# Attention with one filler per head pair on TensorE instead of one per half pair, and score maxima ten pairs ahead

## The chip, the core and the metric

The kernel runs on one core of one Trainium2 chip. The time is the device time of one execution in microseconds (us). The engines of the core run side by side, each through its own list of instructions in order, and wait for one another on semaphores: TensorE (PE; its weight loads are listed as PEld), VectorE (DVE), ScalarE (ACT), GpSimd (POOL) and SyncE (SP), which here only issues DMAs.

## The reference, cut to what matters

The input is x, 32 batches of 256 tokens of width 128. One layer of attention plus a mixture of experts:

```python
xl = _layer_norm(x, ln_l_g, ln_l_b)
xg = _layer_norm(x, ln_g_g, ln_g_b)
# local: attention among the first 32 tokens of each batch (zero for the others)
# glb:   attention among all 256 tokens of each batch
# both: 16 heads of width 8, softmax(q k^T), then times v, then w_out
x = _layernorm(x + (local + glb))
x = _layernorm(x + moe(x))    # top-1 of 8 experts, hidden 512, capacity 1024
```

So the local part is a block of 32 rows for each batch (LW = 32).

## The kernel before

**Units and steps.** The attention is cut into 36 units of 256 query rows: units 0 to 3 are the local part (the 32-row blocks of eight batches each, kept apart by a mask), units 4 to 35 are one batch each. Two units share their input projections; such a pair (18 of them) is projected two pairs ahead. A step u works on unit u, and the program runs steps 0 to 39; the last four only empty the pipeline, and then the experts run (`experts`).

**Head pairs.** The 16 heads of a unit are eight head pairs, hp = 0 to 7, and each pair has two halves e = 0, 1: two heads whose q and k lie in partitions 0 to 63 and 64 to 127. Scores are computed twice. `max_pass` (L513) makes q k^T into `ps_a` (one bank for each e), whose row maxima VectorE takes (`take_max`, L942). `exp_pass` (L536) makes k q^T into `ps_b` with the maximum already subtracted (as extra rows of the operands), ScalarE takes the exponential (`exponential`, L760), and `p_v` (L562) multiplies by v into `ps_o`. q and k are held as sums of bf16 parts stacked to 48 rows, written to memory (`store_stacks`, L329) and read back per unit into `qs` and `ks` (`load_stack`, L358), which have two buffers of 8 pairs each, loaded in halves of four pairs.

**The way of the maxima.** In step u TensorE makes the exponential scores of unit u and the maximum scores of unit u + 1. After four pairs VectorE's maxima are split by GpSimd (`split_max`), turned by TensorE (`turn_max`, L572), copied by ScalarE (`copy_max`, L767, semaphore `mT_ready`) and placed into `qs` by SyncE's DMAs (`place_max`, L384, semaphore `max_rows`); `exp_pass` of pairs 0 and 4 waits for `max_rows`.

**The order on TensorE is written by hand.** Each step is 16 half slots: `score_half(u, hp, e)`, that is two `exp_pass` and two `max_pass` matmuls (which run two at a time, on rows 0 to 63 and 64 to 127 of the array), and then `fill(u, hp, e)`, one piece of other work. The fillers are: `p_v` (a piece of 4 matmuls) after both halves of hp 0, 2, 4 and 6; `turn_x` or `project_in` (inputs of a coming pair) at hp 1 and 5 with `turn_max`; `count_tokens`, `turn_o` at hp 3; `turn_oN`, `turn_x1`, `logits`, `project` at hp 5 and 7. Even steps carry `turn_x` and q, odd steps k and v of the same pair. `max_pass` of a half waits for `take_max` of the pair before in the same half, `exp_pass` for exponentials one or two pairs back.

**The other engines** follow hand-written lists per step too: `fill` on VectorE before each `take_max`, `step` on ScalarE, GpSimd and SyncE. SyncE's list per step before the change is: second half of unit u + 1's stack (4 DMAs), on even steps `store_stacks` (6 DMAs, after waiting for `part2_ready`), `place_max(u, 1)`, `load_xr`, `store_o1` or `store_y`, on even steps `load_x`, first half of unit u + 2's stack (4 DMAs), `place_max(u + 1, 0)`.

## Time and profile before

| | us |
|---|---|
| median of 3 runs (800.12 to 804.97) | 800.67 |
| the profiled execution | 797.34 |
| its span, first to last instruction | 795.4 |
| start of step 0's first exponential | 47.17 |
| steps 0 to 3 (local units) | 47.17 to 109.41 |
| steps 4 to 31 | 109.41 to 570.80 |
| steps 32 to 35 | 570.80 to about 626 |
| emptying and experts | about 626 to 795.4 |
| step 10, step 11 | 15.63, 15.81 |
| step 4, step 8 | 20.53, 22.41 |

A step is counted here from the start of ScalarE's exponential of its pair 0 to that of the next step. Busy shares of the span: PE 87%, PEld 44%, DVE 72%, ACT 62%, POOL 62%. A row of the timeline is: start, duration, engine, line, operation, output<-inputs, shapes, count of merged instructions, and in brackets idle time before it and who ended it. Durations include the instruction's own latency, so the distance between two starts is often shorter than a duration.

### The profile page before, as it was taken

The page shows a single profiled execution, that of the slowest core. Times are in us where ns is not written, and L with a number is a line of the kernel's source. Part 1 is how long each engine was busy: PE and PEld are TensorE (multiplying, and loading weights), DVE is VectorE, ACT ScalarE, POOL GpSimd, SP SyncE. Part 2 cuts the span into 40 slices and gives each one's busy share as a digit, 9 for nine tenths or more (in the row PEclk, how much of TensorE's full clock was granted, in tenths as well). Part 3 has the DMA queues.
Part 4 walks back from the last instruction along what each step waited for, and adds up shares of the span by engine and source line. Part 5 has one row for each costly group of instructions (what it writes and reads, how often), then busy time and mean ns, then how long its engine had stood idle before and what let it go on. Part 6 is the DMA issues. An engine that isn't in the chain of part 4 may idle for free.

```text
span 795.4 us, 19345 instructions
## 1 busy us (share of the span) xinstructions
PE 695.3 (87%) x6502; PEld 351.7 (44%) x6502; DVE 572.3 (72%) x1714; ACT 489.4 (62%) x883; POOL 490.7 (62%) x1004
## 2 busy tenths in 40 slices
PE   1579779898999999899999999999999729999991
PEld 1334333343444444344444444444433415777771
DVE  5555577685888989789888888888887311666664
ACT  1335456585777878678787778787877505344340
POOL 3232324556687877777777768775756650666666
PEclk9755898997999999999999999999999858999996
DMA  4632576756254353352543434525431110343321
GB/s 114 173 107 61 160 193 149 200 137 188 77 166 156 97 174 108 120 176 73 178 145 105 160 104 145 163 70 161 147 95 45 36 57 23 101 132 96 97 73 36
DMA packets 145778, 95.36 MB, mean 120 GB/s; under 512 B 14404, under 2 KB 137885, under 8 KB 145680
## 3 DMA queue, kind: packets, MB, share of 16 engines
q1 hardware_dynamic: 139824, 85.35, 37.0%
q0 software_dynamic: 4096, 7.81, 2.9%
q10 hardware_dynamic: 1760, 0.96, 0.6%
q8 instruction: 53, 0.87, 0.5%
q14 instruction: 45, 0.37, 0.2%
HBM read 47.70 MB, written 45.74 MB: 117 GB/s over the span
## 4 chain that ended last, share of the span: by engine, by line
PE 65%; SPq 13%; DMA 6%; issue 5%; POOL 4%; DVE 4%; ACT 3%; POOLq 0%; ACTq 0%; DVEq 0%
PE ps_b L536 16%; PE ps_o L562 15%; SPq L329 6%; PE ps_a L1382 6%; PE ps_b L1376 5%; SPq L358 4%; DMA qs<-mT 4%; PE ps_f L477 3%; PE ps_f L482 3%; PE ps_f L472 2%; SPq L384 2%; DVE mx L942 2%; POOL out L1496 2%; PE ps_m L572 2%; PE ps_m L606 2%
## 5 line engine op out<-in xcount | busy, mean ns | idle before, releaser
L942 DVE TENSOR_REDUCE mx<-ps_a 128x2 f32<-128x512 f32 (+1 forms) x576 | 374.7, 657 | 109.6 <-PE ps_a L513 102.5
L760 ACT ACTIVATE prob<-ps_b 128x1024 f32<-128x1024 f32 (+1 forms) x288 | 280.7, 975 | 102.5 <-PE ps_b L536 95.0
L536 PE MATMUL ps_b<-qs,ks 59*128 59x256 bf16 (+1 forms) x1152 | 223.3, 276 | 25.7 <-DMA qs<-mT 22.9
L513 PE MATMUL ps_a<-ks,qs 56*128 56x256 bf16 (+1 forms) x1152 | 223.3, 278 | 7.9 <-DVE mx L942 5.0
L562 PE MATMUL ps_o<-prob,vp 128*32 128x256 f32 (+1 forms) x2304 | 183.7, 393 | 0.0
L536 PEld LDWEIGHTS ps_b<-qs,ks 59*128 59x128 bf16 x1152 | 67.0, 95 | 186.2 <-issue 112.2
L1236 POOL DMA_INDIRECT routed<-row,slot x64 | 67.2, 1051 | 31.9 <-issue 26.6
L1496 POOL DMA_INDIRECT out<-res,dest x64 | 64.6, 1010 | 34.2 <-DVE res L1471 19.1
L1172 POOL CAST mpart<-mx 128x16 bf16<-128x16 f32 x72 | 14.0, 194 | 115.2 <-DVE mx L942 114.7
L562 PEld LDWEIGHTS ps_o<-prob,vp 128*32 128x32 f32 x2304 | 46.8, 111 | 61.1 <-issue 54.1
L513 PEld LDWEIGHTS ps_a<-ks,qs 56*128 56x128 bf16 x1152 | 65.2, 96 | 13.4 <-DVE mx L942 8.9
L1421 ACT ACTIVATE prob<-ps_b,b_sb 128x512 f32<-128x512 f32 x48 | 33.0, 687 | 60.2 <-PE ps_b L1376 58.6
L767 ACT COPY mT<-ps_m 24x256 bf16<-24x256 bf16 x72 | 26.0, 361 | 59.2 <-PE ps_m L572 58.8
L1382 PE MATMUL ps_a<-w_sb,prob 128*128 128x128 f32 x512 | 59.6, 276 | 0.0
L1382 PEld LDWEIGHTS ps_a<-w_sb,prob 128*128 128x128 f32 x512 | 58.4, 192 | 0.5 <-issue 0.5
L1154 POOL TENSOR_SCALAR xh<-xt,fmv,frstd 128x128 f32<-128x128 f32 x64 | 50.1, 793 | 1.7 <-issue 0.2
L1209 POOL TENSOR_SCALAR row<-y,mv,rstd 128x128 f32<-128x128 f32 x64 | 50.8, 794 | 0.1
L1376 PE MATMUL ps_b<-xT,w_sb 128*128 128x512 f32 x96 | 46.3, 621 | 0.0
L1452 DVE SCALAR_TENSOR_TENSOR z<-ps_a,rows_sb,xb 128x128 f32<-128x128 f32 x64 | 18.1, 345 | 33.4 <-PE ps_a L1382 33.4
L1186 POOL TENSOR_TENSOR xr<-xr,bo_sb 128x256 f32<-128x256 f32 x36 | 26.1, 724 | 21.7 <-DMA xr<-x 21.6
L1161 POOL TENSOR_TENSOR part<-rest,part 128x512 bf16<-128x512 f32 x32 | 36.4, 1159 | 0.0
L1198 POOL TENSOR_TENSOR rstd<-veps,powm 128x4 f32<-128x4 f32 x32 | 33.3, 1041 | 2.7
(125 smaller groups left out, 1047.8 us busy)
## 6 DMA issues: line engine op xcount, KB each, us to landing
qs<-q_stack SPq DMA_DIRECT2D x144, 96.0 KB
ks<-k_stack SPq DMA_DIRECT2D x144, 96.0 KB
q_stack<-part SPq DMA_DIRECT2D x18, 384.0 KB, 3.0
k_stack<-part SPq DMA_DIRECT2D x18, 384.0 KB, 3.5
q_stack<-part SPq DMA_DIRECT2D x18, 256.0 KB, 3.1
k_stack<-part SPq DMA_DIRECT2D x18, 256.0 KB, 3.6
routed<-empty SPq DMA_DIRECT2D x8, 520.0 KB, 5.7
rows_sb<-routed SPq DMA_DIRECT2D x16, 260.0 KB, 3.8
```

Of the source, the lines that this page charges most:

```text
L329: sp.dma_start(stack[p, :, t0:t0 + n, :], src).then_inc(stack_stored[p % 2], 16)
L513: ins = nc.tensor.matmul(ps_a[:, e, qt * S:qt * S + keys.stop - keys.start], qs[half, h, hp, qt * P:(qt + 1) * P], ks[half, h, hp, keys], ...
L536: ins = nc.tensor.matmul(ps_b[:, exp_bank(hp, e), kt * n:(kt + 1) * n], ks[half, u % 2, hp, kt * P:(kt + 1) * P], qs[half, u % 2, hp, quer ...
L562: last = nc.tensor.matmul(ps_o[32 * j:32 * j + 32, col:col + n], vp[:, u % 6, kt, 4 * q + j, :], prob[:, hp, at:at + n], start=(q % 2 == 0 ...
L760: nc.scalar.activation(prob[:, hp, 0:2 * n].rearrange("p (a n) -> p a n", a=2), src, ACT.Exp).then_inc(exp_done, 1)
L942: nc.vector.reduce_max(mx[:, u % 2, :, col], ps_a[:, e].rearrange("p (t k) -> p t k", t=2)[:, :, 0:k], axis=AX).then_inc(max_done, 1)
L1154: last = nc.gpsimd.tensor_scalar(xh[:, p % 2, t], xt[:, p % 3, t], fmv[:, p % 2, t, 0:1], frstd[:, t:t + 1], ALU.subtract, ALU.mult)
L1209: last = nc.gpsimd.tensor_scalar(row[:, g % 3, t, 0:D], y[:, u % 2, t], mv[:, t, 0:1], rstd[:, 0, t:t + 1], ALU.subtract, ALU.mult)
L1236: pool.indirect_dma_start(out=routed, out_offset=bass.IndirectOffsetOnAxis(ap=slot[:, g % 3, t:t + 1], axis=0), in_=row[:, g % 3, t, :], i ...
L1376: nc.tensor.matmul(ps_h[f], w1_sb[:, he, f * P:(f + 1) * P], xT[:, hk], start=True, stop=True).then_inc(hidden, 1)
L1382: last = nc.tensor.matmul(ps_y[:, bank, t * D:(t + 1) * D], hT[:, hk, f, t * P:(t + 1) * P], w2_sb[:, he, f], start=(f == 0), stop=(f == F ...
L1496: pool.indirect_dma_start(out=out_rows, out_offset=bass.IndirectOffsetOnAxis(ap=dest[:, h, t:t + 1], axis=0), in_=res[:, h, t], in_offset= ...
```

## The change

What it does:

- TensorE: a slot is a whole pair, two `score_half` (8 matmuls) and then one `fill(u, hp)`, which holds the work of two or three of the old fillers. `p_v` pieces are spread over slots 0, 1, 3, 4, 5, 6.
- The maxima run `LEAD = 10` pairs ahead instead of 8, so `max_pass` and `take_max` of unit u + 2's pairs 0 and 1 lie in step u's slots 6 and 7. `qs` and `ks` have three buffers; `load_stack(u + 2)` brings a whole unit in one piece (four DMAs of 192 KB instead of twice four of 96 KB).
- SyncE: `place_max(u, 1)` comes first in a step, then the stack of unit u + 2; `store_stacks` goes to the end of the odd step, behind `place_max(u + 1, 0)`.
- The first half of k is projected in the even step's slot 7, the second half in the odd step's slot 0. `turn_max(u, 1)` is in slot 1, `turn_o` in slot 2, `turn_max(u + 1, 0)` in slot 3, `count_tokens` in slot 5, `turn_oN` and `turn_x1` in slot 6.
- `copy_oNT` and `copy_x1T` are one copy of 512 columns, `copy_turned`. `count_tokens` uses bf16 operands (four matmuls), `queue_places` on GpSimd has two links in place of four, row numbers are set once and moved on by one small instruction.
- VectorE: `norm_o` follows `invert_denominators` in hp 3; the input statistics of a pair are split over an odd and the next even step; other small pieces move by a half slot. ScalarE and GpSimd lists are reordered to match.

```diff
+LEAD = 10
-    qs = sb("qs", [P, 2, NH // 2, S], BF16)
-    ks = sb("ks", [P, 2, NH // 2, S], BF16)
+    qs = sb("qs", [P, 3, NH // 2, S], BF16)
+    ks = sb("ks", [P, 3, NH // 2, S], BF16)
...
+        def load_stack(u):
+
+            b, h, p = u % 3, u % 2, u // 2
+            wait(sp, scores, 8 * (u - 2))
             sp.wait_ge(stack_stored[p % 2], 96 * (p // 2 + 1))
...
         def step(u):
             p = first_pair(u)
-            if there(u + 1):
-                load_stack(u + 1, 1)
-            if u % 2 == 0 and u >= 2 and u // 2 + 1 < NPAIR:
-                store_stacks(u // 2 + 1)
             if there(u):
                 place_max(u, 1)
+            if there(u + 2):
+                load_stack(u + 2)
...
+            if there(u + 1):
+                place_max(u + 1, 0)
+            if u % 2 == 1 and (u + 1) // 2 + 1 < NPAIR:
+                store_stacks((u + 1) // 2 + 1)
...
         def score_half(u, hp, e):
 
+            n = 8 * u + hp + LEAD
             for t in range(2):
                 if there(u):
                     exp_pass(u, hp, 1 - e, t)
-                if there(u + 1):
-                    max_pass(u + 1, hp, e, t)
+                if there(n // 8):
+                    max_pass(n // 8, n % 8, e, t)
...
+        def fill(u, hp):
+
+            first, second = first_pair(u), second_pair(u)
+            if hp == 0:
+                if there(u - 1):
+                    p_v(u - 1, 2, 1)
+                    p_v(u - 1, 3, 0)
+                if second is not None:
+                    project_in(second, "k", 1)
+            if hp == 1:
+                if there(u - 1):
+                    p_v(u - 1, 3, 1)
+                if first is not None:
+                    turn_x(first, 0)
+                    turn_x(first, 1)
...
         for u in range(U + 4):
             for hp in range(8):
-                for e in range(2):
-                    score_half(u, hp, e)
-                    fill(u, hp, e)
+                score_half(u, hp, 0)
+                score_half(u, hp, 1)
+                fill(u, hp)
...
+        def copy_turned(u):
+
+            first, end = (0 if there(u - 1) else S), (2 * S if routes(u - 2) else S)
+            if there(u - 1):
+                act.wait_ge(oN_turned, u)
+                wait(act, projected, u - 1)
+            if routes(u - 2):
+                act.wait_ge(x1_turned, batch(u - 2) + 1)
+                wait(act, logits_ready, batch(u - 2))
+            nc.scalar.copy(turned_T[:, first:end], ps_m[:, first:end]).then_inc(turned_copied, 1)
```

How it moves instructions at three places. First TensorE in an even step of the global units, before: two half slots of one pair and the score matmuls ahead of the second.

```order
L536 MATMUL ps_b<-qs,ks 128x256 [waits exp_done]
L513 MATMUL ps_a<-ks,qs 128x256 [waits max_done]
L536 MATMUL ps_b<-qs,ks 128x256
L513 MATMUL ps_a<-ks,qs 128x256
L562 MATMUL ps_o<-prob,vp 32x256 [waits exp_done]
L562 MATMUL ps_o<-prob,vp 32x256 x3
L536 MATMUL ps_b<-qs,ks 128x256 [waits exp_done]
L513 MATMUL ps_a<-ks,qs 128x256 [waits max_done]
L536 MATMUL ps_b<-qs,ks 128x256
L513 MATMUL ps_a<-ks,qs 128x256
L562 MATMUL ps_o<-prob,vp 32x256 x4
```

And after the change, slot 0 of an even step (L530 is `exp_pass`, L507 `max_pass`, L557 `p_v`).

```order
L530 MATMUL ps_b<-qs,ks 128x256 [waits exp_done,max_rows0]
L507 MATMUL ps_a<-ks,qs 128x256 [waits max_done]
L530 MATMUL ps_b<-qs,ks 128x256
L507 MATMUL ps_a<-ks,qs 128x256
L530 MATMUL ps_b<-qs,ks 128x256 [waits exp_done]
L507 MATMUL ps_a<-ks,qs 128x256 [waits max_done]
L530 MATMUL ps_b<-qs,ks 128x256
L507 MATMUL ps_a<-ks,qs 128x256
L557 MATMUL ps_o<-prob,vp 32x256 x4
L557 MATMUL ps_o<-prob,vp 32x256 [waits exp_done]
L557 MATMUL ps_o<-prob,vp 32x256 x3
```

The two score groups now stand together and the two `p_v` pieces too.

Second SyncE, before, from the middle of an odd step to the middle of an even one (L358 stack loads, L384 the maxima's rows, L329 stack stores).

```order
L358 DMA qs<-q_stack 48x4x256 x2
L358 DMA ks<-k_stack 48x4x256 x2
L384 DMA qs<-mT 3x4x256 x2
L358 DMA qs<-q_stack 48x4x256 x2
L358 DMA ks<-k_stack 48x4x256 x2
L329 DMA q_stack<-part 128x3x512
L329 DMA q_stack<-part 128x2x512
L329 DMA q_stack<-part 128x512
L329 DMA k_stack<-part 128x1536
L329 DMA k_stack<-part 128x1024
L329 DMA k_stack<-part 128x512
L384 DMA qs<-mT 3x4x256 x2
```

After, from the head of an odd step (L380 the maxima's rows, L355 stack loads, L328 stack stores).

```order
L380 DMA qs<-mT 3x4x256 x2
L355 DMA qs<-q_stack 48x8x256 x2
L355 DMA ks<-k_stack 48x8x256 x2
L372 DMA xr<-x_local 32x128
L373 DMA xr<-x 96x128
L374 DMA xr<-x 128x128
L400 DMA out<-o 128x2x128
L380 DMA qs<-mT 3x4x256 x2
L328 DMA q_stack<-part 128x3x512
L328 DMA q_stack<-part 128x2x512
L328 DMA q_stack<-part 128x512
L328 DMA k_stack<-part 128x1536
```

The rows of the maxima no longer stand behind loads and stores; the loads stand behind them.

Third ScalarE in an odd step, before, between the exponentials of pairs 2 and 4 (L735 is `second_part`).

```order
L772 COPY oT<-ps_o 128x512 [waits o_turned,pv_done]
L816 COPY count<-ps_m 128x32 [waits places_ready,counted]
L760 ACTIVATE prob<-ps_b 128x1024 [waits pv_done,scores]
L735 CAST part<-rest 128x2x512 [waits rest_k,rest_q]
L802 COPY row<-tokid 128x2 [waits tok_moved,scattered2]
L804 ACTIVATE tokid<-tokid 128x2 [waits row_numbered]
L760 ACTIVATE prob<-ps_b 128x1024 [waits pv_done,scores]
```

After (L772 is the exponential, L779 `copy_max`, L746 `second_part`).

```order
L784 COPY oT<-ps_o 128x512 [waits o_turned,pv_done]
L779 COPY mT<-ps_m 24x256 [waits max_rows1,max_turned]
L772 ACTIVATE prob<-ps_b 128x1024 [waits pv_done,scores] x2
L779 COPY mT<-ps_m 24x256 [waits max_rows0,max_turned]
L746 CAST part<-rest 128x2x512 [waits rest_k,rest_q]
L812 ACTIVATE row<-row 128x2 [waits row_numbered,scattered0]
L772 ACTIVATE prob<-ps_b 128x1024 [waits pv_done,scores]
```

`copy_max` of the next unit now stands in front of `second_part` between the exponentials of pairs 3 and 4, and waits for TensorE's slot 3.

## Rows read from the trace of the kernel before

**Rows 1.** The page: busy time by engine; shares of the chain that ended last.

```profile
PE 695.3 (87%) x6502; PEld 351.7 (44%) x6502; DVE 572.3 (72%) x1714; ACT 489.4 (62%) x883; POOL 490.7 (62%) x1004
PE 65%; SPq 13%; DMA 6%; issue 5%; POOL 4%; DVE 4%; ACT 3%; POOLq 0%; ACTq 0%; DVEq 0%
```

**Rows 2.** Stretches: length; PE, PEld, DVE, ACT, POOL busy; clock, DMA share, GB/s.

```profile
47.17:109.41 62.24, 55.88 (x577) 26.68 (x581) 37.88 (x96) 31.02 (x62) 22.07 (x50) 0.71 0.37 108
109.41:570.80 461.39, 436.81 (x4516) 194.73 (x4520) 384.00 (x1024) 348.39 (x628) 320.42 (x727) 0.97 0.48 139
180.61:203.02 22.41, 19.24 (x164) 7.64 (x168) 13.39 (x35) 12.24 (x21) 13.33 (x29) 0.77 0.58 173
203.02:218.84 15.82, 15.59 (x168) 7.23 (x172) 14.38 (x44) 12.99 (x26) 11.47 (x27) 1.00 0.28 78
218.84:234.47 15.63, 15.23 (x164) 6.77 (x167) 13.44 (x35) 12.09 (x22) 13.01 (x29) 1.00 0.61 196
585.42:599.64 14.22, 13.56 (x156) 5.71 (x159) 12.54 (x34) 11.03 (x20) 9.05 (x25) 1.00 0.30 85
```

**Rows 3.** Timeline of TensorE, step 15: one half slot between two pieces of p_v.

```profile
301.49 0.28 PE L536 MATMUL ps_b<-qs,ks 59*128 59x256 bf16 x1
...
301.61 0.27 PE L536 MATMUL ps_b<-qs,ks 59*128 59x256 bf16 x1
...
301.81 0.64 PE L562 MATMUL ps_o<-prob,vp 128*32 128x256 f32 x8
302.38 0.28 PE L536 MATMUL ps_b<-qs,ks 59*128 59x256 bf16 x1
```

**Rows 4.** Timeline of TensorE, step 36: pieces of p_v with no scores between.

```profile
626.36 0.86 PE L562 MATMUL ps_o<-prob,vp 128*32 128x256 f32 x12
```

**Rows 5.** Timeline of TensorE, step 15: projections of v followed by turns of two kinds.

```profile
306.29 0.71 PE L472 MATMUL ps_f<-wqkv_sb,xg 128*128 128x128 f32 x4
306.93 0.28 PE L572 MATMUL ps_m<-ident_bf,mpart 128*24 128x128 bf16 x2
...
307.47 0.71 PE L472 MATMUL ps_f<-wqkv_sb,xg 128*128 128x128 f32 x4
308.02 0.38 PE L587 MATMUL ps_m<-ident,oN 128*128 128x128 f32 x2
```

**Rows 6.** Chain that ended last, in step 16: start, length, engine and line.

```profile
312.56 2.10 SPq L358
...
318.71 0.73 SPq L384
...
319.49 1.90 DMA qs<-mT
...
321.43 0.28 PE ps_b L536
```

**Rows 7.** The same chain before step 0: the first half of unit 0's stack.

```profile
30.54 0.32 SPq L358
...
31.88 3.63 DMA ks<-k_stack
```

**Rows 8.** Timeline of VectorE, step 15: statistics, a rest, two maxima one behind the other.

```profile
298.82 0.48 DVE L958 BATCH_NORM_STATS2 stats<-y 128x6 f32<-128x128 f32 x2
...
302.55 0.74 DVE L919 SCALAR_TENSOR_TENSOR rest<-ps_f,bqk_sb,part 128x512 f32<-128x512 f32 x1
303.21 1.28 DVE L942 TENSOR_REDUCE mx<-ps_a 128x2 f32<-128x512 f32 x2
```

**Rows 9.** Timeline of ScalarE, step 15: the second part and the copy of the maxima.

```profile
304.60 1.04 ACT L735 CAST part<-rest 128x1024 bf16<-128x1024 f32 x1
...
307.25 0.36 ACT L767 COPY mT<-ps_m 24x256 bf16<-24x256 bf16 x1 [0.38 <-PE ps_m L572]
```

**Rows 10.** Timeline of GpSimd, step 16: the inputs of a coming pair.

```profile
324.92 3.12 POOL L1154 TENSOR_SCALAR xh<-xt,fmv,frstd 128x128 f32<-128x128 f32 x4
```

**Rows 11.** Transfers in a stretch with much to load: columns as in rows 2.

```profile
324.00:326.00 2.00, 2.00 (x18) 0.71 (x12) 1.02 (x3) 0.56 (x2) 1.90 (x3) 0.71 0.92 267
```

363 lines of the change are left out of this document (174 added, 189 removed).

## The prediction

> **What bounds the kernel now.** I read the page first: TensorE is busy 87% of the span, VectorE 72%, and 13% of the chain that ended last is SyncE issuing, 6% transfers [rows 1]. So two things set the time: TensorE's own list, and waits on something that SyncE issues late. The stretches separate them. An undisturbed odd step takes 15.82 us with TensorE busy 15.59, an undisturbed even one 15.63 with 15.23 [rows 2]: there TensorE bounds, and VectorE (14.38, 13.44) is 1.4 to 2.2 us behind it. Fourteen such pairs of steps would be 14 x 31.45 = 440.3 us, but steps 4 to 31 took 461.39 [rows 2]: 21.1 us are excess. Step 8, at 22.41 with a mean clock of 0.77, is the worst case [rows 2]. The chain in step 16 shows what the excess is: SyncE issues a stack load (one issue took 2.10 us, where its like take 0.3 to 0.5), six stores, and only at 318.71 the rows of the maxima; they land at 321.4 and only then TensorE's pair 4 goes on [rows 6].
>
> **TensorE's list.** One half slot with a piece of p_v takes 302.38 - 301.49 = 0.89: score groups 0.12 apart, 0.20 from the last to p_v, 0.57 to the next score [rows 3]. Two of them are 1.79. Twelve p_v records that follow one another last 0.86, eight last 0.64, so a further phase of four costs 0.22 [rows 3, 4]. A merged slot is therefore 3 x 0.12 (score groups) + 0.20 + 0.57 + 2 x 0.22 = 1.57: 0.22 less. For two other fillers the sum is alike, since what goes is one change from scores to filler and back. Eight of these per step: -1.76.
>
> Part of it is given back where a merged filler mixes shapes. Four projection records take 0.64 when a bf16 turn follows and 0.55 when a 128-wide f32 one follows [rows 5]: a change of shape costs 0.09. Five merged fillers of an even step and four of an odd one mix p_v with 128-wide work: +0.45 and +0.36. The counts in bf16 save some 0.2 a step, an estimate: four f32 records take 0.55 with their follower of the same shape, and two bf16 ones 0.28 with all their latency [rows 5]; it lies between 0 and 0.3. The half of k that moves only shifts 0.45 from odd to even. Work in a pair of steps now: 31.45 less some 0.85 of waits = 30.6. After: 30.6 - 3.5 + 0.8 - 0.4 = 27.5.
>
> The Trainium skill ("TensorEngine Tiling (Array Packing)", Key Properties) says that changing the tiling mode drains TensorE; the 0.09 agrees. If by that rule every change cost half a round trip (0.11), the nine mixed ones would cost 1.0 in place of 0.8, and the pair would be 27.7.
>
> **Which waits come back.** The waits are worked out slot by slot, with T the start of a slot. Both banks of max scores are now filled within 0.36, so VectorE gets its work in bursts. Two maxima in a row last 1.28, one 0.69, so they follow at 0.60 [rows 8]. The first maximum starts at about T + 0.46; the second, with the small work between (f1), ends at T + 0.46 + 0.60 + f1 + 0.72; the next slot's second score group, at T + P + 0.24, waits for it. So a slot must last 1.54 + f1, or more when work before the first maximum (f0) runs over. Slot 0: f1 = 0.47 (two statistics, 0.48 with their latency [rows 8], and a small subtraction), f0 = 0.4 (an addition of the same size and a small maximum), so 2.0 against a TensorE slot of 1.57: +0.5 in even steps, 0 in odd ones, whose slot 0 is long. Slot 2 of even steps has only turn_o (1.2): +0.4; slot 1 of odd ones +0.3; the others 0 to 0.2. Sum +1.6 a pair.
>
> ScalarE, odd steps: its copy of the next unit's maxima needs turn_max at the end of slot 3 and starts at T4 + 0.1; with it (0.32), the second part (0.92 of its 1.04 [rows 9]) and 0.2 for the row numbers, exponential 4 starts 0.85 late, and slot 5's second score group waits +0.8. The single copy of 512 columns before logits: +0.28 in each step (0.56), (0.2 to 0.4; the smaller copy made TensorE wait too). turn_o waits for the bank that copy_max empties, and in odd steps v's first half for the rest of k (0.74 long [rows 8], now in slot 2): +0.4. GpSimd, even steps: the places stand behind the 3.12 us of the coming inputs [rows 10], VectorE's pick in slot 7 waits: +0.25. Together +3.6: the pair is 27.5 + 3.6 = 31.1, against 31.45. Fourteen pairs: **-4.9**. If none of it comes, the pair is 27.5 + 0.5; if every queue adds as much again, 34.
>
> **SyncE's queue.** The rows of the second maxima are ready at T2 + 0.6 (even) or T2 + 1.2 (odd), are issued at once, and land 2.7 later (318.71 to 321.43 [rows 6]): T2 + 3.4 or + 4.0, with slot 4 at T2 + 3.6 or + 4.1. No wait, but no slack. Behind them are four loads of 192 KB. They can begin at T2 + 2.2 (even), + 2.8 (odd); slot 6, the first to read them, stands 7.3 and 7.9 behind T2: 5.1 us. They need about 2 us of issue and landing (1.90 for an almost empty transfer [rows 6]) and 0.79 MB at 267 GB/s [rows 11] = 2.9, so 4.9. Fits by 0.2. Store_stacks ends some 3 us before the next place_max. What stays are single slow issues like that of 2.10 us [rows 6]. I take one such, 1.65 us longer than its like, in every sixth of 28 steps on the critical third of the queue: 8 us. And steps 4 to 7 also clear memory and load weights, about 1 MB each behind which the next rows queue: 6 us. So of 21.1 us excess 14 come back: **-7.1**.
>
> **The rest.** Steps 32 to 35 have no projections; 14.22 each [rows 2], merged 1.76 less, waits +1: **-3**. Steps 0 to 3 took 62.24 at a mean clock of 0.71 (between the levels 1.2 and 2.4 GHz) [rows 2]. Merging gives -1.6 each in 0 to 2 and little in 3, where VectorE is the bound; a 4 us wait in step 2, as in step 16, goes; but slots are shorter, T2 to slot 6 is 5.7, the load has 3.5 us and is 1.3 late in three steps: -5.3 - 3.5 + 3.9 = **-5**. Before step 0 the first half of unit 0's stack landed 5.0 after its first issue (30.54 to 35.51 [rows 7]); a whole one +1.5, and two more pairs of maxima before the first exponential +1: **+2.5**. Masks and memsets of a third buffer lie under the input loads. The emptying steps have shorter place and count chains: **-1**. Experts: unchanged.
>
> Sum: 795.4 - 4.9 - 7.1 - 3 - 5 + 2.5 - 1 = 776.9 of span; its execution is 1.9 longer, and the median shown lies 3.3 above the profiled execution: **782 us**.
>
> **Rivals.**
> (a) TensorE keeps most of its gain: the waits overlap one another and are 1.6 a pair, not 3.6. For it: VectorE's 13.4 to 14.4 is a mean of 1.7 a slot, and a slow slot is followed by fast ones. Then -28 more: 754.
> (b) The loads are late, which makes it slower. A half load of the prologue took 5.0; if the second half adds its 0.39 MB at the 173 GB/s of step 8 [rows 2] it is 7.3, and each global step waits up to 2.2. At +1.2 a step: 782 + 33 = 815. It decides from 0.7 us a step on (18.5 / 28). Against it: 267 GB/s in rows 11, and only 61% of the transfer engines' time needed in rows 2.
> (c) The change doesn't do what it says: waits replace the gain and the excess stays at 21, pair 31.45: 782 + 12 = 794.
> (d) The clock. In step 8, TensorE stood for a wait and ran at the lower level after it (mean 0.77) [rows 2]; if the early waits of 2 us and more persist, three such steps cost 3 us each: 791. The Trainium skill ("TensorE: Matmul & The Clock Gate", HAM oscillation) says that transfer waits of some us between matmuls throttle it again; the row agrees. Without such waits it gives nothing back, as the clean steps are at 1.00.
>
> **How the numbers follow.** Forecast 0.42 (770 to 794), (a) 0.18, (b) 0.20, half of it under 809, (c) 0.12, (d) 0.08. A measurement of this kernel can tell about 1% from no change, 792.7 to 808.7. Faster: most of the forecast, (a), (d), a third of (c): 0.69. Within: 0.19. Slower: 0.12. The range 750 to 808 reaches from just under (a) to (b) at +0.9 a step.
>
> **What would show it.** Pairs of steps from 10 on at 31.1, with p_v pieces 0.22 apart and slots of 1.57; VectorE's wait for max scores shorter in total, TensorE's for VectorE's maxima longer than now, at slots 1 and 3; in odd steps a wait on ScalarE at slot 5. No wait of TensorE for the maxima's rows over 2 us. A wait for the stack loads at slot 6 of most steps would make (b) right; pairs at 29 (a). Wrong altogether would be: shape changes in mixed fillers at much over 0.09, or a first exponential past 52.

## The result, and the profile after

The changed kernel takes 872.09 us (median of 4 executions, 869.23 to 879.96) where the kernel before took 800.39 beside it: ratio 1.095, interval 1.089 to 1.102. Slower by some 72 us, where 782 us was forecast. The profiled execution is the longest of the four, with a span of 878.1 us.

The page of the changed kernel: busy time by engine, and the chain that ended last by engine and by line ([rows 1] are their like of before).

```profile
PE 697.3 (79%) x6502; PEld 391.1 (45%) x6502; DVE 573.8 (65%) x1716; ACT 477.9 (54%) x820; POOL 474.7 (54%) x908
PE 46%; DMA 24%; SPq 8%; DVE 6%; issue 6%; POOL 5%; ACT 4%; ACTq 0%; POOLq 0%; DVEq 0%
DMA ks<-k_stack 22%; PE ps_o L557 9%; PE ps_b L530 7%; PE ps_a L507 6%; SPq L355 6%; PE ps_a L1395 4%; PE ps_b L1389 3%; PE ps_m L588 3%; PE ps_m L601 3%; POOL out L1509 3%; DVE mx L951 2%; PE ps_f L476 2%; PE ps_m L582 2%; ACT prob L772 2%; DVE rest L928 1%
```

TensorE's share of the chain fell from 65% to 46%, transfers rose from 6% to 24%, and 22 of these 24 are one thing: the stack load, `ks<-k_stack`. TensorE's busy time did not fall either: 697.3 for 695.3.

The list of waits of the changed kernel: engine, line, what it waited for, us in total, how often, the longest.

```profile
ACT prob L772 <- PE ps_b L530: 202.1, 184, 5.7
DVE mx L951 <- PE ps_a L507: 176.6, 199, 6.0
PE ps_a L507 <- DMA ks<-k_stack: 85.0, 35, 6.4
```

At slot 6, where the first maximum scores of unit u + 2 stand, TensorE waited for their load in each of steps 0 to 33, and once before step 0 (6.4 us): 35 times, 2.4 us in the mean. VectorE and ScalarE wait behind it.

Stretches of the changed kernel, columns as in [rows 2]: steps 4 to 31; steps 9 to 31; steps 0 to 3; step 16, a slow one; step 25, one with the clock at 1.00.

```profile
121.18:642.72 521.54, 441.23 (x4516) 228.86 (x4520) 385.35 (x1031) 339.72 (x573) 307.48 (x652) 0.90 0.55 123
214.32:642.72 428.40, 363.55 (x3730) 189.72 (x3733) 319.36 (x873) 281.57 (x485) 264.46 (x559) 0.90 0.51 116
50.07:121.18 71.11, 53.17 (x579) 30.05 (x581) 37.20 (x89) 30.70 (x62) 22.22 (x50) 0.69 0.52 116
348.70:371.19 22.49, 19.30 (x166) 9.61 (x170) 14.17 (x42) 11.93 (x20) 13.35 (x27) 0.73 0.38 69
517.63:534.31 16.68, 13.85 (x166) 7.47 (x169) 13.73 (x37) 12.53 (x23) 10.53 (x24) 1.00 0.66 166
```

Steps 4 to 31 took 521.54 for 461.39 [rows 2]. The mean granted clock is 0.90 of full speed there, 0.97 before; in step 16 it is 0.73, so part of that step ran at the lower of the two levels (1.2 GHz), behind a wait of 3 us at slot 6. The whole loss of span, 82.7 us, by parts: before step 0's exponential +2.9, steps 0 to 3 +8.9, steps 4 to 31 +60.2, steps 32 to 35 +12.7, the rest -2.0.

The chain in step 26 of the changed kernel: start, length, what.

```profile
539.90 0.22 SPq L355
...
541.18 6.02 DMA ks<-k_stack
547.20 0.05 issue
547.25 0.28 PE ps_a L507
```

The first of the four DMAs of the load is issued at 539.75, the last at 541.18, and all have landed at 547.20: 7.45 us. In steps 9 to 31 a load took 6.6 to 8.3 us from first issue to landing, 7.15 in the median. In the 6 us from 541.20 on the transfer engines are full, and moved 168 GB/s:

```profile
541.20:547.20 6.00, 3.88 (x49) 1.78 (x48) 3.33 (x12) 3.17 (x6) 4.84 (x9) 1.00 1.07 168
```

### The profile page after: what moved, and what is told of

It reads as the page before. It is cut to its first block, busy times and chain, and to the rows that moved or that the text cites. A ratio compares the mean times of both kernels' runs of the same rounds, so it can differ in the third digit from the quotient of the medians.

```text
span 878.1 us, 19003 instructions
## 1 busy us (share of the span) xinstructions
PE 697.3 (79%) x6502; PEld 391.1 (45%) x6502; DVE 573.8 (65%) x1716; ACT 477.9 (54%) x820; POOL 474.7 (54%) x908
## 4 chain that ended last, share of the span: by engine, by line
PE 46%; DMA 24%; SPq 8%; DVE 6%; issue 6%; POOL 5%; ACT 4%; ACTq 0%; POOLq 0%; DVEq 0%
DMA ks<-k_stack 22%; PE ps_o L557 9%; PE ps_b L530 7%; PE ps_a L507 6%; SPq L355 6%; PE ps_a L1395 4%; PE ps_b L1389 3%; PE ps_m L588 3%; PE ps_m L601 3%; POOL out L1509 3%; DVE mx L951 2%; PE ps_f L476 2%; PE ps_m L582 2%; ACT prob L772 2%; DVE rest L928 1%
## 5 line engine op out<-in xcount | busy, mean ns | idle before, releaser
L951 DVE TENSOR_REDUCE mx<-ps_a 128x2 f32<-128x512 f32 (+1 forms) x576 | 365.1, 657 | 177.5 <-PE ps_a L507 176.6
L772 ACT ACTIVATE prob<-ps_b 128x1024 f32<-128x1024 f32 (+1 forms) x288 | 280.4, 974 | 204.6 <-PE ps_b L530 202.1
L507 PE MATMUL ps_a<-ks,qs 56*128 56x256 bf16 (+1 forms) x1152 | 199.5, 298 | 90.8 <-DMA ks<-k_stack 85.0
L530 PE MATMUL ps_b<-qs,ks 59*128 59x256 bf16 (+1 forms) x1152 | 214.4, 294 | 18.0 <-ACT prob L772 13.5
L557 PE MATMUL ps_o<-prob,vp 128*32 128x256 f32 (+1 forms) x2304 | 181.5, 416 | 0.0
L530 PEld LDWEIGHTS ps_b<-qs,ks 59*128 59x128 bf16 x1152 | 92.1, 102 | 105.0 <-ACT prob L772 46.1
L507 PEld LDWEIGHTS ps_a<-ks,qs 56*128 56x128 bf16 x1152 | 81.6, 102 | 111.2 <-DMA ks<-k_stack 91.5
L557 PEld LDWEIGHTS ps_o<-prob,vp 128*32 128x32 f32 x2304 | 56.9, 117 | 65.1 <-issue 55.3
L1395 PEld LDWEIGHTS ps_a<-w_sb,prob 128*128 128x128 f32 x512 | 58.5, 192 | 0.5 <-issue 0.5
L1158 POOL TENSOR_TENSOR frstd<-fveps,powm 128x4 f32<-128x4 f32 x18 | 18.5, 1029 | 48.9 <-DVE fveps L917 48.9
L779 ACT COPY mT<-ps_m 24x256 bf16<-24x256 bf16 x72 | 25.9, 359 | 31.6 <-PE ps_m L567 31.6
```

The source lines that it names most:

```text
L507: ins = nc.tensor.matmul(ps_a[:, e, qt * S:qt * S + keys.stop - keys.start], qs[half, b, hp, qt * P:(qt + 1) * P], ks[half, b, hp, keys], ...
L530: ins = nc.tensor.matmul(ps_b[:, exp_bank(hp, e), kt * n:(kt + 1) * n], ks[half, u % 3, hp, kt * P:(kt + 1) * P], qs[half, u % 3, hp, quer ...
L557: last = nc.tensor.matmul(ps_o[32 * j:32 * j + 32, col:col + n], vp[:, u % 6, kt, 4 * q + j, :], prob[:, hp, at:at + n], start=(q % 2 == 0 ...
L772: nc.scalar.activation(prob[:, hp, 0:2 * n].rearrange("p (a n) -> p a n", a=2), src, ACT.Exp).then_inc(exp_done, 1)
L951: nc.vector.reduce_max(mx[:, u % 2, :, col], ps_a[:, e].rearrange("p (t k) -> p t k", t=2)[:, :, 0:k], axis=AX).then_inc(max_done, 1)
L1395: last = nc.tensor.matmul(ps_y[:, bank, t * D:(t + 1) * D], hT[:, hk, f, t * P:(t + 1) * P], w2_sb[:, he, f], start=(f == 0), stop=(f == F ...
```

## The experiments

Runs are called by the number in their label. In all of them the kernel before ran on the same chip; its median there was 798 to 814 us, so ratios are what compares. A step's length is taken as in the table of before, from one first exponential to the next.

**Runs 1 to 3: what makes the load late.** Edits of SyncE's list and of the load.

```diff
# e1_load_first: SyncE, step
-            if there(u):
-                place_max(u, 1)
             if there(u + 2):
                 load_stack(u + 2)
             if there(u):
+                place_max(u, 1)
```

> Edit: in SyncE's step the stack load of unit u + 2 stands ahead of place_max(u, 1); nothing else. Theory L (the loads reach slot 6 late because they start behind the rows of the maxima, about 2.1 us after slot 2 begins, and take 7.4 us): they now start with the step, some 6 us earlier, so TensorE's wait for the stack at slot 6 (85 us in 35 waits in the changed kernel) falls under 5 us, the granted clock returns to 0.93 or more, and the time is 770 to 795. Theory C (the lower clock comes from the way the slots bunch the matmuls, whatever the loads do): the wait goes but the mean clock stays at 0.87 to 0.89, time 800 to 830. Theory S (the merged slots themselves are slower): steps without a wait at slot 6 still take over 16 us, time over 800 at a good clock.

Measured: 827.57 us, ratio 1.031 (1.023 to 1.039). The wait for the load is gone, and another took its place:

```profile
PE ps_a L507 <- DMA ks<-k_stack: 7.0, 1, 7.0
PE ps_b L530 <- DMA qs<-mT: 48.8, 20, 8.5
SPq L355 <- PE ps_b L530: 97.3, 18, 8.1
SPq L343 <- DMA k_stack<-part: 21.3, 8, 4.1
```

SyncE now stands at the head of a step for the scores that still read the buffer, or in even steps for the stores of the stack, and the second max rows queue behind it. In step 22 they were late enough for 20.67 us; the odd steps around it took 15.3 to 15.5. None of the three theories is met as it was put: the wait went, as L said, but the time lies above L's range and the mean clock rose to 0.915 only.

```diff
# e2_halves: load_stack in two halves of four pairs, each with its own semaphore
-            if hp == 0 and e == 0 and qt == 0:
+            if hp % 4 == 0 and e == 0 and qt == 0:
-                pe.wait_ge(stack_loaded[b], 64 * (u // 3 + 1) + extra)
+                pe.wait_ge(stack_loaded[b][hp // 4], 64 * (u // 3 + 1) + extra)
```

> Edit: the load stays behind place_max(u, 1) but is cut into two halves of four DMAs with a semaphore each, the first four pairs first; pair 0 waits for the first half alone. Theory L: the first half lands some 4 to 5 us after its first issue in place of 7.4, so most of the 85 us of waits at slot 6 goes (under 20 us left), time 785 to 815. If the late start alone matters and not the size of the piece, the waits stay above 60 us and the time near 860.

Measured: 805.56 us, ratio 1.004 (1.001 to 1.008).

```profile
PE ps_a L509 <- DMA ks<-k_stack: 8.9, 6, 3.5
PE ps_b L532 <- DMA qs<-mT: 30.0, 25, 4.3
```

The same bytes, at the same place in SyncE's list, and nearly the whole loss is back (1.095 to 1.004). In steps 9 to 31 of this run a half lands 4.3 us after its first issue in the median, and both halves 6.4 us after the first issue of the first, for 7.15 of the whole load. So the eight smaller DMAs are even some 0.8 us faster together, but that is little beside the other effect: pair 0 at slot 6 needs only the first half, and pair 4 comes four slots later.

```diff
# e3_xr_late: SyncE, step
             if there(u + 2):
                 load_stack(u + 2)
+            if there(u + 1):
+                place_max(u + 1, 0)
             if there(u):
                 load_xr(u)
...
-            if there(u + 1):
-                place_max(u + 1, 0)
```

> Edit: load_xr and store_o1 or store_y go behind place_max(u + 1, 0), so that the stack load has the transfer engines for itself for some us. If the 7.4 us of a load are made long by the 0.18 MB of xr and o1 issued right behind it, landing falls to about 6 us and the waits by some 30 us: time 825 to 845. If the load is limited by its own descriptors, nothing changes: within 1% of 872.

Measured: 892.14 us, ratio 1.110 (1.101 to 1.119), the waits for the load 81.4 us (85.0 in the changed kernel). A load took 7.1 us in the median of steps 9 to 31, as before, so the small transfers behind it do not delay it. The time met neither forecast: the order cost a further 20 us, with a mean clock of 0.851 for 0.865. Why is open.

**Run 4: half the bytes.** From unit 3 on this kernel loads pairs 0 to 3 of a unit only, so it leaves out half of the stack loads.

```diff
# e4_half_bytes
-                    sp.dma_start(dst[HALF * e:HALF * e + STACK, b], src[e]).then_inc(stack_loaded[b], 16)
+                    n = NH // 2 if u < 3 else NH // 4
+                    sp.dma_start(dst[HALF * e:HALF * e + STACK, b, 0:n], src[e][:, 0:n]).then_inc(stack_loaded[b], 16)
```

> Edit: from unit 3 on, only pairs 0 to 3 of each stack are loaded (the others keep what an earlier unit left), so half of the loaded bytes are left out and the result is another. It measures the price of the bytes: if landing time follows them, a load lands about 4.5 us after its first issue, the waits at slot 6 go and the time is 775 to 800; if it is the latency of four issues on a busy queue, the wait stays over 1 us a step and the time over 840.

Measured: 786.46 us, ratio 0.981 (0.973 to 0.989). The waits for the load are 16.6 us, 6 times, all early, and the clock is at 1.00 in the steady steps. A load lands 4.1 us after its first issue here (median of steps 9 to 31). This bounds what the load costs, at some 86 us (872.1 less 786.5; 92 by the two ratios). With run 2 it says that the load's size against its window is the cause, not the merged slots.

**Run 6: the window.** One number.

```diff
# e6_lead9
-LEAD = 10
+LEAD = 9
```

> The changed kernel with one number altered: the maxima run nine pairs ahead and not ten, so the first reader of a unit's stacks stands one slot (about 2 us) later, and nothing else moves. Theory L (each step waits because the load lands some 9.5 us after the step's second max rows are turned, and the reader comes at 7): the waits of the max matmuls for the stacks fall by about 2 us times 33, from 85 us to 20 to 35, TensorE's mean clock rises from 0.865 to above 0.90, and the time is 815 to 840. Rival C (the wait is contention among transfers, and moves with the reader): waits stay at 70 us or more and the time over 855.

Measured: 820.23 us, ratio 1.022 (1.016 to 1.028), waits for the load:

```profile
PE ps_a L507 <- DMA ks<-k_stack: 18.3, 13, 4.4
```

The reader is 2 us later and the waits fall by 67 us, which is 2 us in each of 33 steps. Together the runs show one cause from four sides: bytes, pieces, place and reader. The kernel is still slower than run 2 by 1.8%, and the waits for the load are not why. In every even step from 14 to 30 the clock was low at the head of the step, as here in step 18:

```profile
349.17:351.00 1.83, 1.83 (x17) 0.59 (x16) 1.83 (x9) 1.13 (x2) 1.53 (x2) 0.50 0.15 49
351.00:353.00 2.00, 2.00 (x22) 0.82 (x19) 1.28 (x5) 0.89 (x1) 1.78 (x4) 0.61 0.13 39
```

and no wait of TensorE ahead of it was over 0.8 us.

**Run 5: the queue behind it.** The first max rows between the halves, everything else of the step behind both.

```diff
# e5_between: SyncE, step
             if there(u + 2):
-                load_stack(u + 2)
+                load_stack(u + 2, (0,))
+            if there(u + 1):
+                place_max(u + 1, 0)
+            if there(u + 2):
+                load_stack(u + 2, (1,))
             if there(u):
                 load_xr(u)
...
```

> The load of a unit in halves, as in the earlier run with two halves (805.6 us, ratio 1.004), but the first max rows of the next unit are sent between the two halves, and x's rows for the residual, o1 and y behind the second. Theory Q (what is left of the loss is SyncE's queue: eight loads in one block hold up the max rows that come behind them): the waits of the exponential score matmuls for max rows fall from 30 us to under 12, steps 2 to 8 of 18.6 to 21.7 us come under 17, and the time is 785 to 795. Rival M (the slots of whole pairs are no shorter than the half slots were, and the queue costs nothing more): the steps from 10 on stay at 16.0 to 16.5 us and the time at 798 to 808. A wait for the second half at slot 2 of a step, of 1 us or more, would say that the load is now sent too late.

Measured: 802.62 us, ratio 0.999 (0.996 to 1.002). The waits for max rows fell, to 18.7 us in 7 places, but steps 4, 6 and 8 kept 21.8, 21.2 and 21.1 us, so theory Q is wrong for these, and the time and most steps from 10 on are where rival M put them. The chain in step 4 of this run shows what stands ahead of the rows:

```profile
110.94 0.47 SPq L396
...
111.45 0.89 SPq L396
...
112.39 1.44 SPq L382
...
113.87 4.78 DMA qs<-mT
118.65 0.05 issue
118.69 0.39 PE ps_b L534
```

L396 are two clears of 520 KB each, L382 the max rows of 6 KB. In step 16 of the kernel before such rows landed in 1.90 us [rows 6], here in 4.78; in steps 6 and 8 of this run it is 5.15 and 4.53, in steps 9 to 31 1.9.

**Runs 7 and 8: the prediction's terms for the slots.** Both start from run 5.

```diff
# e7_split_fill: TensorE
                 score_half(u, hp, 0)
+                fill_pv(u, hp)
                 score_half(u, hp, 1)
                 fill(u, hp)
```

> As the run with the max rows between two half loads, but a slot's p_v matmuls stand between its two half slots of scores and only the rest of the filler behind them: so twice the number of changes between score matmuls and others in the six slots with both, as before the change. Theory S (the prediction's term: a slot of a whole pair saves 0.22 us of issue): the time rises against that run by 0.2 us for each of 6 slots in 32 steps, about 35 to 45 us. Rival N (the extra issue time is hidden behind VectorE and ScalarE, which a slot waits for anyway): the two are within 1%, under 8 us apart.

Measured: 847.97 us, ratio 1.056 (1.051 to 1.061): 45 us more than run 5. As theory S said, the time is up by more than 35 us. But the run doesn't show that a change saved is worth 0.2 us. In steps 9 to 31 (392.5 us for 371.9) TensorE was busy 341.9 us for 338.7 and idle 50.6 for 33.1: most of what was lost there is waiting, above all for exponentials, which p_v needs half a slot sooner in this order. What a change costs is seen in slots without a wait. Slot 4 of step 20, first in run 5, then in run 7:

```profile
386.22 0.28 PE L534 MATMUL ps_b<-qs,ks 59*128 59x256 bf16 x1
...
388.39 0.28 PE L534 MATMUL ps_b<-qs,ks 59*128 59x256 bf16 x1
```

```profile
402.24 0.28 PE L534 MATMUL ps_b<-qs,ks 59*128 59x256 bf16 x1
...
404.52 0.28 PE L534 MATMUL ps_b<-qs,ks 59*128 59x256 bf16 x1
```

That is 2.17 and 2.28 us: 0.11 for one more change. Slot 5 of even steps (1.30 and 1.41) and slots 0 and 3 of odd ones (2.17 and 2.28, 1.97 and 2.07, the shortest of each) say the same. The prediction took 0.22 for such a change less 0.09 for the mixed shapes, so 0.13. Slots with p_v alone have no more changes than before the edit, and stay at 1.55. In the profiled executions the rest of the loss stands in steps 0 to 8 (7.4 us), in steps 32 to 35 (7.6) and around them (3.6).

```diff
# e8_part_late: ScalarE, step
-            if second is not None:
-                second_part(second)
...
             if there(u):
                 exponential(u, 4)
+            if second is not None:
+                second_part(second)
```

> As the run with the max rows between two half loads, but in odd steps ScalarE's copy of the stacks' second part comes behind exponential 4 instead of ahead of it. Theory A (the prediction's term: this copy makes exponential 4 of odd steps about 0.8 us late, and the score matmuls behind it): the distance from exponential 3 to 4 in odd steps falls from 2.7 us to about 1.9, that from 4 to 5 grows by less, an odd step gets 0.5 to 0.9 us shorter, and the time 8 to 14 us less. Rival: the copy is only moved to a slot that waits as long for it (VectorE's third part and the stores of the stacks come later), the odd step keeps its length and the time is within 0.5%.

Measured: 811.43 us, ratio 1.010 (1.006 to 1.013). The distance of exponentials 3 and 4 in odd steps fell from 2.74 to 1.97 as forecast, and that of 4 and 5 rose from 1.48 to 2.17, that from 7 to the next step from 2.08 to 2.87. The rival holds: the delay is real, but moved it only waits elsewhere, and the odd step got longer.

**Runs 9, 11, 12, 14, 15, 17, 18: steps 4, 6 and 8.** The clears and the first two experts' weights at other places.

```diff
# e12_clears_even: SyncE, step; e17 moves the weights only, e18 the clears only
-            if LU - 1 <= u < LU + 3:
+            if u in (0, 2, 4, 6):
                 clear_routed(u)
-            if u == LU + 3:
-                tail.first_weights(sp)
+            if u in (8, 10):
+                tail.first_weights(sp, (u - 8) // 2)
```

> As the run with the max rows between two half loads, but 7 of the 8 transfers of 520 KB that clear the list of routed rows are sent before the first step, while SyncE would stand idle, the eighth at the end of step 4, and the two first experts' weights at the ends of steps 6 and 8 and not both at the end of step 7. Theory K (the waits for the second max rows in steps 4, 6 and 8, of 4.5 to 6 us each, come from these big transfers ahead of them in the queues: the rows were sent at 112.4 us and landed at 118.7 behind 1 MB of clears): steps 4, 6 and 8 fall from 21.8, 21.2 and 21.1 us to 16 to 17, the waits for max rows to under 6 us in all, and the time from 802.6 to 785 to 790. Rival: the rows are late by their own few small descriptors or by SyncE, the three steps keep 20 us or more, and the time stays within 4 us of 802.

> As the run with the max rows between two half loads, but the eight clears go out two at a time at the ends of steps 0, 2, 4 and 6 (behind which no stores of stacks and 10 us of idle queue follow) and the first two experts' weights at the ends of steps 8 and 10. Sent before the first step, the clears had made steps 6 and 8 15.2 and 15.5 us long, where 21.2 and 21.1 stood, and the first exponential 13 us later. Theory K: here steps 4, 6 and 8 come to 15 to 17 us with the first exponential still at 47 us, so the time falls by 12 to 16 us against that run, to 0.98 to 0.985 of the kernel before. Rival: the big transfers hold up some other step by as much wherever they stand (steps 1, 3, 5, 7 grow by 3 us or more), and the ratio stays at 0.995 to 1.0.

> As the run with the max rows between two half loads (clears at the ends of steps 3 to 6), and only the first experts' weights moved, to the ends of steps 8 and 10. Theory K: step 8 falls from 21.1 us to 15 to 16, steps 4 and 6 stay near 21. The steady steps (9 to 31) hold the same instructions in both runs with clears at even steps, where they took 362 to 363 us, and in the run with max rows between the halves, where they took 372. If that difference belongs to the program, to where the weights go, these steps take 362 to 365 us here; if it belongs to the chip or the run, this kernel and the next of this list agree with each other within 3 us, at either level; if to the clears, they take 370 or more here and 363 in the next.

> As the run with the max rows between two half loads, and only the clears moved, two at the ends of each of steps 0, 2, 4 and 6; the weights stay at the end of step 7. Theory K: steps 4 and 6 fall from 21.8 and 21.2 us to 15 to 17, step 8 stays at 20 or more, step 5 takes over one wait. Steps 9 to 31 as said of the run before it: 370 us or more if the weights decide, 363 if the clears do.

Measured: with the clears before the first step 810.13 us, ratio 0.998 (0.994 to 1.002); its steps 6 and 8 fell to 15.2 and 15.5, but TensorE waited 15.8 us for unit 0's stack, which SyncE sends behind the clears, and the first exponential came at 60.6, for 47.2. At even steps: 779.91 us, ratio 0.982 (0.975 to 0.989). Weights only: 782.93, ratio 0.982 (0.978 to 0.986). Clears only: 783.95, ratio 0.983 (0.980 to 0.987). First steps 4, 6 and 8 with the weights moved only, then steps 4, 5, 6 and 8 with the clears moved only:

```profile
105.99:128.82 22.83, 16.51 (x156) 7.73 (x160) 12.38 (x28) 10.77 (x14) 7.22 (x15) 0.77 0.72 193
143.23:165.59 22.36, 17.13 (x162) 7.99 (x166) 13.25 (x33) 11.57 (x17) 10.22 (x22) 0.85 0.92 220
180.80:196.63 15.83, 14.91 (x163) 7.33 (x161) 14.02 (x42) 11.75 (x19) 12.81 (x27) 1.00 0.56 180
```

```profile
110.93:126.36 15.43, 14.03 (x153) 6.82 (x153) 12.18 (x28) 10.69 (x14) 6.52 (x14) 0.93 0.51 166
126.36:147.25 20.89, 15.31 (x157) 7.21 (x160) 12.27 (x23) 11.62 (x19) 5.30 (x12) 0.84 0.80 206
147.25:162.45 15.20, 14.58 (x162) 7.32 (x166) 13.19 (x33) 11.45 (x16) 9.92 (x21) 1.00 0.32 92
178.53:199.62 21.09, 16.36 (x154) 7.79 (x154) 13.19 (x39) 11.66 (x19) 13.41 (x27) 0.84 0.62 181
```

The clears hold up steps 4 and 6, the weights step 8. In run 5 clears stand at the ends of steps 3 to 6, and steps 5 and 7 are not long; what sets 4 and 6 apart is that the six stores of the stacks, 1.5 MB, are sent just before the clears. At their new place two clears hold up step 5 (20.89), and step 1 takes 16.2 us for 11.5. One clear at the end of each of steps 0 to 7 was the test of that:

> As the run with two clears at the ends of steps 0, 2, 4 and 6 (779.9 us, 0.982 of the kernel before), but one clear of 520 KB at the end of each of the steps 0 to 7. There, step 5 had taken over the wait: 21.1 us, with the second max rows 5.4 us late behind the 1 MB sent at the end of step 4. If a queue full of big transfers is all there is to it, halving them takes step 5 to 15 to 18 us without bringing steps 6 and 8 back to 21, and the time to 774 to 779, ratio 0.972 to 0.98. If the wait only wanders (another step of 3 to 8 at 20 us or more), the time stays at 778 to 784.

Measured: 785.11 us, ratio 0.981 (0.975 to 0.988). Step 5 fell to 17.0, and step 8, which has nothing of the weights ahead of it in this run but the eighth clear, took 23.2. The wait wanders, as the second reading said.

The same moves on the kernel before:

> The kernel before with the clears and the first weights moved in the same way (weights at the ends of steps 5 and 7), nothing else. If theory K is right, its steps 4, 6 and 8 (20.5, 19.9 and 22.4 us) fall to 16 to 17 too and the time to 786 to 793, ratio 0.980 to 0.988, so that the whole of such a gain is none of the merged slots' doing. If these waits belong to the changed order alone, nothing moves.

> The kernel before with the clears at the ends of steps 0, 2, 4 and 6 and the weights at those of 8 and 10, nothing else. If theory K is right for it too, steps 4, 6 and 8 (20.5, 19.9, 22.4 us) fall to 16 to 17 and the ratio is 0.982 to 0.988, about the same as the merged version's; then merged slots, with their loads mended, are worth nothing or less. If the ratio stays above 0.995, the earlier position was not what held the rows up here.

Measured: clears before the first step 818.9 us, ratio 1.007 (1.003 to 1.011). At even steps 790.0 us, ratio 0.995 (0.991 to 1.000), steps 4, 6 and 8 at 19.3, 16.0 and 15.3. So theory K is right for the kernel before too, in steps 6 and 8, but it earned half a per cent there and not the 1.2 to 1.8 that I expected: one step, 22, was 20.96 us long in its profile, and steps 0 to 3 took 66.1 us for 62.2.

**Runs 10, 13, 16: what bounds the steady steps.** Three small moves; 10 starts from 9, 13 from 12, 16 from 15.

```diff
# e10_places_late: VectorE: beyond_capacity and pick_slot to the next step's slot 0
# e13_k_slot1: TensorE, fill: second half of k from hp 0 to hp 1 (ScalarE's first part of k moves with it, behind exponential 1)
-                if second is not None:
-                    project_in(second, "k", 1)
             if hp == 1:
                 if there(u - 1):
                     p_v(u - 1, 3, 1)
+                if second is not None:
+                    project_in(second, "k", 1)
# e16_xr_early: SyncE, step: load_xr ahead of load_stack(u + 2, (1,))
```

> As the run with the clears sent first, but VectorE's sum that picks a token's place waits half a slot later and the two operations that make the slot number of it come at the next step's start. Theory V (in even steps VectorE stands 0.5 us in the last slot for GpSimd's product of places, and the score matmuls behind it in slots 7 and 0 are late by that): the even steps of 16.2 us get 0.3 to 0.6 us shorter and the time falls by 4 to 8 us. Rival: VectorE's own work at the start of a step (maxima, residual, statistics) is the limit there, the moved operations are added to it, and the time is the same within 0.5% or longer.

> As the run before it in this list, but the second half of k's projection stands in slot 1 of an odd step and not in slot 0, and ScalarE's first part of k behind exponential 1 and not 0. Theory P (slot 0 of odd steps, 2.7 us from exponential to exponential, is bound by TensorE, with 16 p_v and 2 projection matmuls in it): slot 0 falls to 2.2, slot 1 grows from 1.7 to about 2.0, and an odd step is 0.2 us shorter, 3 us in all. Rival V (the slot is bound by VectorE: residual, logits and statistics between the maxima): slot 0 stays at 2.5 or more, slot 1 grows by 0.3, and the time is 3 to 6 us longer.

> As the run before it in this list, but the rows of x for the residual are sent ahead of the second half of the stack load and not behind it. In the runs with the load in halves GpSimd waits 32 times, 59 to 64 us in all, for these rows at the end of a step, and its addition to them then falls together with VectorE's slot arithmetic: of 32 such operations 10 or 11 overlap it and take 0.37 us in the mean where 0.16 us stand alone, and 3 or 4 of the next take 0.58 us for 0.16. If this clash delays the score matmuls of slots 7 and 0, the operations are back at 0.16 us, GpSimd's wait falls under 20 us, and the time is 3 to 6 us less. If it is hidden, the same within 0.5%; and if the second half of the load now lands late, max matmuls wait for it at slot 2.

Measured: 819.25 us, ratio 1.007 (1.004 to 1.011), for 0.998 without the move; 786.84, ratio 0.992 (0.988 to 0.996), for 0.982; 786.38, ratio 0.984 (0.979 to 0.990), for 0.981. The first two rivals hold: slot 0 is not helped by less work in slot 7, and k in slot 1 makes slot 1 2.61 us long for 1.63 (in step 17 the scores there wait 0.25 us for VectorE's maximum) while slot 0 gains 0.35. In the third GpSimd's wait for the rows fell from 62.5 to 16.1 us, but now 20 of VectorE's 32 operations met its addition, not 9; at 0.30 us in the mean for 0.16 they cost nothing that can be measured.

## Why the prediction was wrong, by its own steps

The parts of the span, in us, from the profiled executions; "mended" is run 17: loads in halves, the first max rows between them, the weights moved.

| | before | after | run 2 | run 4 | run 5 | mended |
|---|---|---|---|---|---|---|
| step 0's first exponential | 47.2 | 50.1 | 47.3 | 50.1 | 47.2 | 47.5 |
| steps 0 to 3 | 62.2 | 71.1 | 66.0 | 61.3 | 59.3 | 58.5 |
| steps 4 to 8 | 93.6 | 93.1 | 91.2 | 81.8 | 94.9 | 90.6 |
| steps 9 to 31 | 367.8 | 428.4 | 375.1 | 365.4 | 371.9 | 361.3 |
| steps 32 to 35 | 55.3 | 68.1 | 57.5 | 59.0 | 60.4 | 55.7 |

**The step that failed: "So 4.9. Fits by 0.2."** The load takes 7.15 us in the median (7.45 in step 26), not 4.9. The terms beside it held: the first issue stands 2.1 us (even steps) and 2.9 us (odd) behind the start of slot 2, for 2.2 and 2.8, and slot 6 starts at 7.1 and 8.0, for 7.3 and 7.9 (medians of steps 10 to 31). The text took one rate, 267 GB/s, from 2 us of the kernel before in which several kinds of transfer ran together [rows 11], and put a whole load on it. While a load lands the rate is 168 GB/s, although the transfer engines are as full as there and the packets as large (2,074 packets and 1.01 MB in 6.00 us; 1,081 and 0.53 MB in the 2.00 us of rows 11). So a packet takes longer, and why is not shown. The kernel before held the better measure: its halves of 0.39 MB took 5.8 and 3.9 us in step 16, and 5.0 in [rows 7]; the one of 5.8, from 322.68 to 328.44, even spans the 2 us from which the rate was taken. Two of them in a row are not 4.9 (6.4 in run 2). Rival (b) took 173 GB/s and said 7.3 us and up to 2.2 of wait. Measured are 7.15, and waits of 1.3 to 3.0 us in steps 9 to 31, 1.9 in the mean.

**Why it cost more than rival (b) said.** It and rival (d) were priced apart, and here they multiply. In steps 9 to 31 TensorE waited 43.9 us for the load. It was also busy for 363.55 us with the work that takes it 330.86 in the mended run:

```profile
196.63:557.93 361.30, 330.86 (x3747) 170.27 (x3746) 320.58 (x878) 280.98 (x485) 263.18 (x558) 1.00 0.44 137
```

at a mean granted clock of 0.90 against 1.00. So the waits cost 43.9 us and the lower clock 32.7 of busy time; together that is 76.6, of which 67 show in the length. The text had put three steps at 3 us each on the clock. The Trainium skill ("TensorE: Matmul & The Clock Gate", HAM oscillation) says that waits of some us between matmuls throttle TensorE again; the trace agrees, though not step by step. The mean clock was 0.73 to 0.95 in 17 of these 23 steps. It fell to the lower level 12 times, each time during or within 2 us behind a wait for the load, of 1.4 to 3.0 us; behind the other 11 such waits, of 1.3 to 2.2 us, it did not fall. Nearly without waits for the load, the mean clock of these steps was 0.99 in run 2 and 1.00 in runs 4 and 5, but 0.96 in run 6. The condition of (d), waits of 2 us and more, was met by (b) in 9 of the 23 steps, and the text had not joined the two.

**The slots: right in the rows.** A merged slot with 16 records of p_v was put at 1.57. In step 25 of the changed kernel it is 526.32 - 524.77 = 1.55:

```profile
524.77 0.28 PE L530 MATMUL ps_b<-qs,ks 59*128 59x256 bf16 x1
...
525.32 1.07 PE L557 MATMUL ps_o<-prob,vp 128*32 128x256 f32 x16
526.32 0.28 PE L530 MATMUL ps_b<-qs,ks 59*128 59x256 bf16 x1
```

In slots with other work beside p_v, run 7 gives 0.11 us for a change where 0.13 was taken. The waits that were to come back are at their places in the same step: 0.54 for the exponential in slot 5 (0.8 forecast), 0.35 for the rest of k and 0.35 for ScalarE's copy before the logits (0.4 and 0.28):

```profile
521.76 0.68 PE L466 MATMUL ps_f<-wqkv_sb,xg 128*128 128x128 f32 x4 [0.35 <-DVE rest L928]
527.25 0.28 PE L530 MATMUL ps_b<-qs,ks 59*128 59x256 bf16 x1 [0.54 <-ACT prob L772]
532.60 0.58 PE L601 MATMUL ps_m<-wg_sb,turned_T 128*128 128x8 f32 x4 [0.35 <-ACT turned_T L795]
```

VectorE's waits did not come where the text had them: in run 17 slots 0 and 2 of even steps and slot 1 of odd ones take 1.55, 1.13 and 1.21 us on TensorE, where 2.0, 1.6 and about 1.5 were expected. Slot 1 of even steps is long instead (2.48 us, where the shortest of the changed kernel is 1.91).

**The steady pair: right as a sum, by luck in its parts.** Forecast 31.1. The median even and odd steps from 10 on sum to 31.2 in the mended run (15.81 + 15.39) and 31.25 in run 12. But TensorE is busy 28.8 us a pair there (330.86 / 11.5) where 27.5 was put, and idle 2.6 where 3.6 was, so two errors of about 1 us cancel. And it is 32.3 in run 5 and 31.9 in run 4, with the same instructions on TensorE and the clock at 1.00 in all. The levels seem to follow the program, as far as one profiled execution of each tells: runs 5 and 15 were made on the same chip and differ (371.9 and 363.0 us for steps 9 to 31), runs 12, 15 and 17 on three chips agree within 1.7. Where they part is slots 0 to 2: 2.64, 1.70 and 2.12 us of an odd step in run 5, 2.42, 1.63 and 1.87 in run 12 (medians). In slot 2 of every odd step from 10 on TensorE waits some 0.3 us for VectorE's maximum in run 5, in all but one of them in run 4, and never in runs 12, 15 and 17. Moving the weights of steps 7 to 10 should not change a step 20, and what does is open. Of the 1.7% by which the mended version beats run 5, this is 10 us and step 8 some 5.

**SyncE's excess, -7.1.** The text expected that max rows ahead of everything would be in time and kept 14 us for slow issues, clears and weights. In run 5 steps 4, 6 and 8 stood at 64.1 us, where they take 45.1 with clears and weights moved (run 12): 19 us, and the text had counted 6 for them. But step 5 grew by 6.7 in run 12 and steps 0 to 3 by 4.2, so over steps 0 to 8 it gained only 8.5. In the kernel before they were 62.8 together, so none of that came back until the big transfers were moved. From step 9 on the excess was only 6 us in the kernel before (367.8 for 11.5 pairs of 31.45), less than the 7.1 that the term wanted back.

**The rest.** Before step 0: +2.9 for +2.5. Steps 0 to 3: forecast -5, measured +8.9; with the loads mended -3.0 in run 5 and -3.7 in 17, but +3.8 in run 2 and +1.3 in 12. Steps 32 to 35: forecast -3, measured +12.7, mended +0.4. I had taken the merged gain there whole; steps 32 and 33 are 14.6 to 15.8 and 14.2 to 14.5 us in runs 12, 15 and 17, no shorter than those of before (14.6 and 14.2). Emptying and experts: -1 forecast, -2.0 measured.

**A version faster than both.** Experiment 12: loads in halves, the first max rows between them, clears at even steps, weights at 8 and 10. 779.91 us, 1.8% less than the kernel before (0.975 to 0.989). That this is near the 782 of the forecast is chance: it moves clears and weights, which the change does not, and with them where they were (run 5) the mended change is worth nothing (0.999). With the same clears and weights the kernel before is at 0.995; so of the 1.8% some 1.3 belong to the change with its loads mended, if the two ratios, of one chip, are set against each other. How much of that is the merged slots alone was not tested.

## What to carry to other kernels

When a load is moved into a tighter window, take its time from a load of the same kind in the trace, first issue to landing, and not from bytes over the best rate that some stretch shows; and give a load in as many pieces as it has readers at different times, each with its own semaphore. A wait that comes once in every step is not priced alone: ask what the clock does behind it, since here 44 us of waits took 33 us of slower matmuls with them. In a queue that serves in order, look for the few large transfers ahead of the small urgent one; moving them shifts the wait to whatever comes behind, so put them where nothing urgent follows.
